# Graph-network kernel: bounded scatters, loads issued ahead of the store, merged one-hots, and message parts kept as upper halves of 32-bit words

## The chip, the cores and the metric

The kernel runs on one core of one Trainium2 chip, as one launch. The metric is the device time of that launch in microseconds (us), as the median of several runs. The engines are PE (TensorE, with PEld for its weight loads), DVE (VectorE), ACT (ScalarE), POOL (GpSimd) and SP (SyncE, which here only issues DMAs).

## The reference, cut to what matters

Four graph layers run one after the other on 6250 nodes of 64 features, each followed by adding to the residual and a layer norm. The 206250 edges (`src`, `dst`) come sorted by `dst`.

```python
# layer 0: hypergraph convolution, twice (relu between): gather, segment sum by edge index, gather, segment sum by node
# layer 1 (pass 4 of the kernel):
h = relu(concat([edges, nodes[receivers], nodes[senders]]) @ We1 + be1)     # one row of 128 per edge
agg = segment_sum(h @ We2 + be2, receivers)
new_nodes = relu(concat([agg, nodes]) @ Wn1 + bn1) @ Wn2 + bn2
# layer 2 (pass 5):
msg = sigmoid(k[dst] + q[src]) * v[src]                                     # one row of 64 per edge
out = segment_sum(msg, dst) + x @ W_skip + b_skip
# layer 3 (pass 6): normalized neighbour sum
```

All of it is float32. The kernel multiplies on PE in bfloat16, with each float32 value split into three bfloat16 parts (high, middle, low) whose products are added in float32.

## The kernel before, in words

The nodes are 49 blocks of 128. A **window** is the block of 128 target nodes whose edges are handled together; there are 49 (`NB`). In each window every edge gets a **slot**: a source block (49 of them) and a place 0 to 127 in it. So gathers and segment sums become matmuls with one-hot matrices of 128 x 128. A **chunk** is seven source blocks (`CH` = 7), so a window has seven chunks (`NC` = 7) and a pass 343.

The stages, in order of time:

1. **Placing the edges** (`place_edges`), window by window: DVE compares and ranks, PE counts, ACT copies. It leaves in `SD` and `slot_rows` the source and target number of every slot, and in `sidx_w` the row of DRAM tensor `feat_slot` to which each edge's features go.
2. **Counts** (`make_counts`): for each chunk DVE builds two one-hots from `sd4` (`one_hots`, L1768 to L1774, two instructions), PE multiplies them into two count matrices (L988), ACT and DVE copy these out (L1343, L1347, L1783), and SP stores them to DRAM (`cnt_t`, `cnt_s`), 3.1 MB a window.
3. **Layer 0**: three products with those counts, loaded again by SP (L519) through a ring of seven buffers (L1052, L1089).
4. **Pass 4** (layer 1) and **pass 5** (layer 2), both by `slots(k)`, with a node stage after each.
5. **Pass 6**: one more product of the counts, and the end.

**The scatters.** `feat_slot` is 307328 rows of 64 floats, filled with zeros by seven DMAs of SP (L490) while the edges are placed. Beside stages 1 to 3 POOL brings the edge features in: per window four loads of nine features for each of 128 partitions (`fetch`, L731, 288 KB each, two buffers) and 36 indirect DMAs (L753), each of which scatters 128 rows of 256 bytes to `feat_slot`. Nothing limits how many are in flight. A `fetch` into a buffer waits until all scatters out of it have landed; it stands after the third scatter of a chunk of nine. Ahead of window 10 POOL waits for the last count matrix (L775). The scatters count up two semaphores, one for each buffer. Pass 4 needs window w of `feat_slot` before its window w (L553).

**One chunk of a slot pass.** SP loads the slot numbers of the chunk, repeated to all 128 partitions, into `selS[c]` and `selT[c]` (L559), in pass 4 also the features `fslot[c]` (L562). DVE turns the two into one-hots in place (`select_rows`, L1951, L1952) and builds a third, `sumT[c]`, the other way round (`select_sums`, L1965). PE transposes the features (L1120, pass 4) and adds up in PSUM, per source block, three products with `selS` and three with `selT` (`meet`, L1137, L1141), in pass 4 also two of the features (L1148). Then the messages are made and split. In pass 4: ACT writes relu of PSUM twice, as float32 in `hid` and as bfloat16, the high part, in `parts3` (L1434, L1435); DVE subtracts (`residual`, L1985); ACT converts the rest, the middle part (L1443); DVE subtracts again, the low part (`last_part`, L1995). In pass 5: ACT's sigmoid (L1438), DVE's product (`gate`, L1979), ACT's high part (L1441), DVE's residual, ACT's middle part, and the low part on POOL (L685). At last PE adds the three parts by target, seven matmuls of 384 or 192 columns (`add_up`, L1161). PE's loop runs `transpose` for chunk c, `meet` for chunk c-2 and `add_up` for chunk c-4; DVE handles the messages of chunk c-2 around the one-hots of chunk c. Once a window ACT and DVE add the two halves of the sum into `ystage` (L1449, L2004 to L2008) and SP stores it (L567).

**The order on SP** in a slot pass is written out: all loads of window w, each behind the semaphore that says that `meet` of the same chunk of window w-1 is done, then the store of window w-1, which waits for DVE's last addition, then the next window's loads:

```python
load(0)
with sp.Fori(1, NB) as w:
    load(w)
    store(w - 1)
store(NB - 1)
```

## Time and profile before

| | us |
|---|---|
| median of three timed runs | 5509.07 |
| lowest and highest | 5475.67, 5522.33 |
| span of the profiled execution | 7358.4 |
| another time of the profiled execution | none recorded |
| PE busy in the span | 4866.3 (66%) |
| DVE, ACT, POOL busy | 3454.7, 2501.9, 2368.3 |

The span is one execution taken by the hardware profiler. It is a third longer than the timed runs, so its stretches have to be read one by one before a duration is carried over to them. "Busy" is time in which an engine executes instructions; waits, branches and the issue of DMAs are not in it.

### The profile page before, as it was taken

Reading aid. Unit: us, or ns where it says so; the run is one execution under the profiler, and the core shown is the slowest. Engines: PE = TensorE matmul, PEld = TensorE weight load, DVE = VectorE, ACT = ScalarE, POOL = GpSimd, SP = SyncE. Lnnn points to the kernel's source line nnn. Section 1 sums busy time; section 2 is a strip of 40 time slices with the busy share of each in tenths; the row PEclk is TensorE's granted clock in tenths of the full one; section 3 lists DMA queues with packets and bytes.
Section 4 is the critical chain, followed back from the end, with each engine's and each line's share of the span. In section 5 each row is a group of like instructions: output and inputs, shape, how many; then the busy total and the mean of one; then the engine's idle time right before and its main releaser. Section 6 shows DMA issues by size and latency. Waiting matters only on the chain.

```text
span 7358.4 us, 157880 instructions
## 1 busy us (share of the span) xinstructions
PE 4866.3 (66%) x61948; PEld 4161.5 (57%) x61948; DVE 3454.7 (47%) x5668; ACT 2501.9 (34%) x3821; POOL 2368.3 (32%) x2387
## 2 busy tenths in 40 slices
PE   2773599623332223328959999999999758877857
PEld 2662488511220112117948888878878657777757
DVE  7992488200000000001046666666666468888842
ACT  1332499200000000000035555555555345555520
POOL 0787400577777777771000000000000013333310
PEclk9666799755555555558979999999999779999989
DMA  7963477722332222327933343443433144444457
GB/s 150 222 140 103 165 290 287 236 74 89 108 111 75 81 88 93 110 88 312 389 123 118 125 132 116 129 129 114 135 122 121 46 157 144 141 144 148 150 193 306
DMA packets 802722, 1103.68 MB, mean 150 GB/s; under 512 B 428155, under 2 KB 708081, under 8 KB 794988
## 3 DMA queue, kind: packets, MB, share of 16 engines
q1 hardware_dynamic: 721658, 986.29, 41.0%
q0 software_dynamic: 73696, 111.71, 5.3%
q8 instruction: 270, 4.42, 0.2%
q10 hardware_dynamic: 7056, 0.91, 0.1%
q14 instruction: 42, 0.34, 0.0%
HBM read 788.30 MB, written 314.35 MB: 150 GB/s over the span
## 4 chain that ended last, share of the span: by engine, by line
PE 35%; issue 26%; another core or an unknown queue 13%; DVE 9%; ACT 5%; DMA 5%; POOL 4%; SPq 2%; DVEq 0%; POOLq 0%; ACTq 0%
PE PS L1052 8%; POOL arena L685 4%; PE PS L1137 4%; PE PS L1141 4%; PE PS L1161 4%; PE PS L1089 4%; PE PS L1148 4%; DMA arena<-feat_slot 3%; PE PS L988 2%; PE PS L1120 2%; DVE arena L1726 1%; ACT arena L1343 1%; PE PS L827 1%; ACT arena L1347 1%
## 5 line engine op out<-in xcount | busy, mean ns | idle before, releaser
L753 POOL DMA_INDIRECT feat_slot<-SK,sidx_p x1764 | 1855.7, 1052 | 1060.5 <-issue 1039.8
L1137 PE MATMUL PS<-arena 128*128 128x128 bf16 x14406 | 1471.6, 222 | 271.6 <-DVE arena L1965 269.2
L1052 PE MATMUL PS<-arena 128*128 128x192 bf16 (+1 forms) x7203 | 832.8, 266 | 1028.1 <-issue 908.2
L1141 PE MATMUL PS<-arena 128*128 (+2 forms) x14406 | 1437.7, 209 | 1.9
L685 POOL TENSOR_TENSOR arena<-arena 128x448 bf16<-128x448 f32 x343 | 360.6, 1051 | 3349.2 <-ACT arena L1443 3349.2
L1052 PEld LDWEIGHTS PS<-arena 128*128 128x128 bf16 x7203 | 648.4, 103 | 1213.5 <-issue 1099.1
L1137 PEld LDWEIGHTS PS<-arena 128*128 128x128 bf16 x14406 | 976.9, 99 | 348.9 <-issue 170.6
L1141 PEld LDWEIGHTS PS<-arena 128*128 128x128 bf16 x14406 | 971.9, 100 | 4.3
L1985 DVE TENSOR_TENSOR arena<-arena 128x896 f32<-128x896 f32 (+1 forms) x686 | 588.3, 858 | 544.9 <-ACT arena L1435 540.1
L1443 ACT ACTIVATE arena<-arena 128x896 bf16<-128x896 f32 (+1 forms) x686 | 523.8, 764 | 634.4 <-DVE arena L1985 634.4
L1161 PE MATMUL PS<-arena 128*128 128x384 bf16 (+1 forms) x4802 | 705.8, 287 | 7.8 <-POOL arena L685 4.0
L1089 PE MATMUL PS<-arena 128*128 128x192 bf16 x2401 | 289.2, 266 | 368.4 <-issue 367.8
L988 PE MATMUL PS<-arena 128*128 128x128 bf16 x4802 | 363.0, 226 | 221.4 <-ACT arena L1343 125.7
L1161 PEld LDWEIGHTS PS<-arena 128*128 128x128 bf16 x4802 | 392.6, 98 | 162.0 <-DVE arena L1995 4.6
L1862 DVE TENSOR_SCALAR arena<-PS 128x448 f32<-128x448 f32 x7 | 4.4, 625 | 1002.0 <-remote 643.9
L1089 PEld LDWEIGHTS PS<-arena 128*128 128x128 bf16 x2401 | 214.0, 103 | 443.6 <-issue 441.8
L988 PEld LDWEIGHTS PS<-arena 128*128 128x128 bf16 x4802 | 300.5, 101 | 273.4 <-issue 110.7
L1995 DVE TENSOR_TENSOR arena<-arena 128x896 bf16<-128x896 f32 x343 | 374.6, 1092 | 147.2 <-ACT arena L1443 142.8
L1965 DVE TENSOR_TENSOR arena<-sd,iota 128x896 bf16<-128x896 bf16 x686 | 424.8, 619 | 3.4
L1833 DVE TENSOR_REDUCE arena<-PS 128x128 f32<-128x384 f32 (+1 forms) x84 | 38.5, 505 | 820.6 <-PE PS L1052 499.8
L1148 PE MATMUL PS<-wtwo,arena 64*128 64x128 f32 x4802 | 399.6, 287 | 0.0
L1343 ACT ACTIVATE arena<-PS 128x896 bf16<-128x896 f32 x343 | 311.6, 927 | 215.3 <-remote 159.4
(238 smaller groups left out, 6438.0 us busy)
## 6 DMA issues: line engine op xcount, KB each, us to landing
arena<-slot_rows SPq DMA_DIRECT2D x1372, 224.0 KB, 4.5
arena<-cnt_t SPq DMA_DIRECT2D x147, 896.0 KB
arena<-cnt_t SPq DMA_DIRECT2D x147, 672.0 KB
feat_slot<-zero SPq DMA_DIRECT2D x7, 10976.0 KB, 54.0
cnt_t<-arena SPq DMA_DIRECT2D x49, 1568.0 KB
cnt_s<-arena SPq DMA_DIRECT2D x49, 1568.0 KB
arena<-feat_slot SPq DMA_DIRECT2D x343, 224.0 KB, 5.1
SK<-in_edge_attr_dram POOLq DMA_DIRECT2D x196, 288.0 KB
```

Source lines behind the costliest of these rows:

```text
L685: pool.tensor_tensor(parts3[i][:, 2 * n:3 * n], hid[i][:, 0:n], parts3[i][:, n:2 * n], ALU.subtract)\
L753: pool.indirect_dma_start(feat_slot, bass.IndirectOffsetOnAxis(ap=sidx_p[odd][:, n:n + 1].bitcast(u32), axis=0), fwin[h][:, t * D:(t + 1) ...
L988: last = nc.tensor.matmul(to[:, cut], one[:, cut], two[:, cut], start=True, stop=True)
L1052: last = nc.tensor.matmul(PS[:, at:at + w3], ring[u % RING][:, of:of + P], esplit[:, (i * CH + w) * w3:(i * CH + w + 1) * w3], start=u == ...
L1089: last = nc.tensor.matmul(PS[:, i * 512:i * 512 + w3], ring[u % RING][:, of:of + P], psplit2[:, b * w3:(b + 1) * w3], start=b == 0, stop=b ...
L1137: last = nc.tensor.matmul(PS[:, to:to + P], selS[c][:, cut], qsplit[:, (b * 3 + s) * H:(b * 3 + s + 1) * H], start=s == 0 and (k != 4 or j ...
L1141: last = nc.tensor.matmul(PS[:, to:to + w_], selT[c][:, cut], dsplit[:, bass.ds(w * (3 * w_) + s * w_, w_)], start=False, stop=k != 4 and ...
L1148: last = nc.tensor.matmul(PS[:, to:to + P], fT[i][rows, pair_of[j] * P:(pair_of[j] + 1) * P], wtwo[rows, :], start=False, stop=True, skip_ ...
L1161: last = nc.tensor.matmul(o, sumT[c][:, j * P:(j + 1) * P], parts[:, :, place_of[j] if k == 4 else j, :], start=c in (0, 4) and j == 0, st ...
L1443: nc.scalar.activation(parts3[i][:, n:2 * n], hid[i][:, 0:n], ACT.Copy).then_inc(msg_mid, 1)
L1965: V.tensor_tensor(sumT[c].rearrange("p (b s a) -> p b s a", b=CH, a=4), sum4[:, c * CH * 4:(c + 1) * CH * 4].rearrange("p (b s a) -> p b s ...
L1985: V.tensor_tensor(hid[i][:, 0:CH * w_], hid[i][:, 0:CH * w_], parts3[i][:, 0:CH * w_], ALU.subtract)\
```

## The change

The edits fall into five groups.

**Scatters.** At most `LIVE` = 4 are in flight: scatter n of a window counts up semaphore n % 4 and waits ahead of that for the scatter before it on the same semaphore. `fetch` stands after the fifth scatter of nine and waits for the same scatters as before. The wait for the count matrices ahead of window 10 is gone. The zero fill writes rows of 448 floats out of a wider `zero` tile instead of 64.

**One-hots of the counts.** The slots are kept in the order (chunk, source or target, block) instead of (source or target, chunk, block), so that both one-hots of a chunk are neighbours and one DVE instruction makes them.

**Slot loads.** By the same order both slot rows of a chunk come in one DMA into `sel_c[c]` (3.5 KB a partition), and one DVE instruction makes one-hots of them.

**Order on SP.** Two windows are loaded first; from then on the store of window w-2 is issued after the fifth chunk's load of window w.

**Message parts.** `hid` has room for three float32 parts. Each part is read as the upper 16 bits of its float32 words (`upper`, a bfloat16 view with a step of two), so no converting copy is made: ACT writes the message (relu) or its gate once, DVE subtracts the upper half of part 1 to get part 2, and DVE or POOL the upper half of part 2 to get part 3. PE reads the `upper` view as its moving operand in `add_up`.

```diff
+LIVE = 4
+PUTS = WT // LIVE
+ZW = 448
+PAIR = 2 * CH
@@ tiles
-        ohs_c = [carve(19 + 1.75 * c, CH * P, bf16) for c in range(NC)]
-        oht_c = [carve(31.25 + 1.75 * c, CH * P, bf16) for c in range(NC)]
+        hot_c = [carve(19 + 3.5 * c, PAIR * P, bf16) for c in range(NC)]
+        ohs_c = [hot[:, 0:CH * P] for hot in hot_c]
+        oht_c = [hot[:, CH * P:PAIR * P] for hot in hot_c]
-        selS = [carve(73.5 + 1.75 * c, CH * P, bf16) for c in range(NC)]
-        selT = [carve(85.75 + 1.75 * c, CH * P, bf16) for c in range(NC)]
+        sel_c = [carve(73.5 + 3.5 * c, PAIR * P, bf16) for c in range(NC)]
+        selS = [sel[:, 0:CH * P] for sel in sel_c]
+        selT = [sel[:, CH * P:PAIR * P] for sel in sel_c]
-        hid = [carve(122.5 + 8.75 * i, CH * P) for i in range(2)]
-        parts3 = [carve(126 + 8.75 * i, 3 * CH * P, bf16) for i in range(2)]
+        hid = [carve(122.5 + 10.5 * i, 3 * CH * P) for i in range(2)]
+        upper = [h.bitcast(bf16).rearrange("p (n two) -> p n two", two=2)[:, :, 1] for h in hid]
@@ SP, zero fill
-                sp.dma_start(z, zero[:, 0:D].rearrange("p (a f) -> p a f", a=1).to_broadcast((P, FROWS // NC // P, D)))\
+                sp.dma_start(z, zero[:, :].rearrange("p (a f) -> p a f", a=1).to_broadcast((P, rows, ZW)))\
@@ SP, slots
-                def load(w):
-                    if k == 4:
-                        for h in range(2):
-                            sp.wait_ge(feat_put[h], w * (FCH // 2 * FT * 16) + FCH // 2 * FT * 16)
+                def load(w, between=None):
                     for c in range(NC):
-                        if not isinstance(w, int):
+                        if not isinstance(w, int) or w > 0:
                             sp.wait_ge(pre_made, w * NC + (m * GB + c + 1 - NC))
-                        for kk, to in ((0, selS[c]), (1, selT[c])):
-                            row = slot_rows[bass.ds(w, 1), kk * NB + c * CH:kk * NB + (c + 1) * CH, :]
-                            sp.dma_start(to, row.rearrange("a k s -> a (k s)").to_broadcast((P, CH * P))).then_inc(slot_in[c], 16)
+                        rows = slot_rows[bass.ds(w, 1), c * PAIR:(c + 1) * PAIR, :]
+                        sp.dma_start(sel_c[c], rows.rearrange("a k s -> a (k s)").to_broadcast((P, PAIR * P))).then_inc(slot_in[c], 16)
                         if k == 4:
+                            if c == 0:
+                                for i in range(LIVE):
+                                    sp.wait_ge(feat_put[i], w * (PUTS * 16) + PUTS * 16)
...
+                        if between is not None and c == 4:
+                            store(between)
...
                 load(0)
-                with sp.Fori(1, NB) as w:
-                    load(w)
-                    store(w - 1)
+                load(1)
+                with sp.Fori(2, NB) as w:
+                    load(w, w - 2)
+                store(NB - 2)
                 store(NB - 1)
@@ POOL, last part of pass 5
-                        pool.wait_ge(msg_mid, w * NC + (GB + c + 1))
-                        pool.tensor_tensor(parts3[i][:, 2 * n:3 * n], hid[i][:, 0:n], parts3[i][:, n:2 * n], ALU.subtract)\
+                        pool.wait_ge(msg_res, w * NC + (GB + c + 1))
+                        pool.tensor_tensor(hid[i][:, 2 * n:3 * n], hid[i][:, n:2 * n], upper[i][:, n:2 * n], ALU.subtract)\
@@ POOL, put_features
                         n = c * FT + t
+                        i = n % LIVE
+                        if not isinstance(w, int) or w > 0 or n >= LIVE:
+                            pool.wait_ge(feat_put[i], w * (PUTS * 16) + n // LIVE * 16)
+                            pool.nop(nofuse=True)
                         pool.indirect_dma_start(
...
-                            .then_inc(feat_put[h], 16)
-                        if t == 2 and c < FCH - 1:
+                            .then_inc(feat_put[i], 16)
+                        if t == 4 and c < FCH - 1:
                             fetch(w, c + 1)
...
-            with pool.Fori(3, 5) as i:
-                put_features(i * 2, 0)
-                put_features(i * 2 + 1, 1)
-            pool.wait_ge(cs_made, NB * NC)
-            with pool.Fori(5, NB // 2) as i:
+            with pool.Fori(3, NB // 2) as i:
@@ PE, add_up
-                    parts = parts3[(c + odd) % 2][:, 0:3 * CH * w_].rearrange("p (s j f) -> p s j f", s=3, j=CH)
+                    parts = upper[(c + odd) % 2][:, 0:3 * CH * w_].rearrange("p (s j f) -> p s j f", s=3, j=CH)
@@ ACT, messages
                     if k == 4:
-                        nc.scalar.activation(hid[i], PS[:, at:at + CH * P], ACT.Relu).then_inc(msg_made, 1)
-                        nc.scalar.activation(parts3[i][:, 0:n], PS[:, at:at + CH * P], ACT.Relu).then_inc(pre_free, 1)
+                        nc.scalar.activation(hid[i][:, 0:n], PS[:, at:at + CH * P], ACT.Relu).then_inc(pre_free, 1)
...
-                        act.wait_ge(pre_free, w * NC + (GB + c + 1))
-                        nc.scalar.activation(parts3[i][:, 0:n], hid[i][:, 0:n], ACT.Copy).then_inc(msg_hi, 1)
-                    act.wait_ge(msg_res, w * NC + (m * GB + c + 1))
-                    nc.scalar.activation(parts3[i][:, n:2 * n], hid[i][:, 0:n], ACT.Copy).then_inc(msg_mid, 1)
@@ DVE, make_counts
-                    for k, to in ((0, ohs_c[c]), (1, oht_c[c])):
...
+                    V.tensor_tensor(
+                        hot_c[c].rearrange("p (b s a) -> p b s a", b=PAIR, a=4),
...
@@ DVE, slots
-                    V.tensor_scalar(selS[c], selS[c], pnum1[:, 0:1], None, ALU.is_equal)
-                    V.tensor_scalar(selT[c], selT[c], pnum1[:, 0:1], None, ALU.is_equal)
+                    V.tensor_scalar(sel_c[c], sel_c[c], pnum1[:, 0:1], None, ALU.is_equal)
...
-                    dve.wait_ge(*((pre_free, w * NC + (c + 1)) if k == 4 else (msg_hi, w * NC + (c + 1))))
-                    V.tensor_tensor(hid[i][:, 0:CH * w_], hid[i][:, 0:CH * w_], parts3[i][:, 0:CH * w_], ALU.subtract)\
-                        .then_inc(msg_res, 1)
+                    dve.wait_ge(pre_free, w * NC + (m * GB + c + 1))
+                    V.tensor_tensor(hid[i][:, n:2 * n], hid[i][:, 0:n], upper[i][:, 0:n], ALU.subtract).then_inc(msg_res, 1)
...
-                    dve.wait_ge(msg_mid, w * NC + (m * GB + c + 1))
-                    V.tensor_tensor(parts3[i][:, 2 * n:3 * n], hid[i][:, 0:n], parts3[i][:, n:2 * n], ALU.subtract)\
+                    dve.wait_ge(msg_res, w * NC + (m * GB + c + 1))
+                    V.tensor_tensor(hid[i][:, 2 * n:3 * n], hid[i][:, n:2 * n], upper[i][:, n:2 * n], ALU.subtract)\
```

## Rows read from the trace of the kernel before

**Rows 1.** The profile page: its head.

```profile
span 7358.4 us, 157880 instructions
```

**Rows 2.** Busy time by stretch: stretch, length, then busy us of each engine.

```profile
0.00:556.00 556.00, 327.83 (x4321) 268.23 (x4321) 498.78 (x573) 161.82 (x491) 314.43 (x226) 0.78 0.77 170
556.00:840.00 284.00, 81.67 (x711) 67.27 (x712) 49.16 (x85) 54.49 (x66) 211.19 (x222) 0.58 0.30 94
840.00:1331.00 491.00, 461.72 (x6488) 425.11 (x6485) 437.86 (x749) 460.71 (x573) 0.14 (x1) 0.99 0.73 288
1331.00:3683.00 2352.00, 950.95 (x7342) 687.68 (x7343) 95.92 (x228) 30.50 (x50) 1481.99 (x1597) 0.61 0.42 140
3816.00:5740.00 1924.00, 1794.05 (x22706) 1559.24 (x22707) 1234.14 (x1886) 1112.11 (x1403) 0.00 (x0) 0.97 0.40 126
5952.00:7060.00 1108.00, 879.74 (x16807) 804.37 (x16807) 916.60 (x1911) 566.20 (x1079) 360.59 (x343) 0.99 0.46 144
```

**Rows 3.** Busy time by stretch of line 988 alone (PE, PEld, clock, DMA).

```profile
840.00:1331.00 491.00, 309.50 (x4318) 258.40 (x4315) 0.99 0.73 288
```

**Rows 4.** Busy time in the last product, which runs beside nothing.

```profile
7120.00:7320.00 200.00, 200.00 (x2390) 199.67 (x2391) 16.47 (x36) 4.76 (x10) 0.00 (x0) 0.99 0.96 386
```

**Rows 5.** Timeline of pass 4 (start, us, engine, line; idle before), and PE's waits.

```profile
4632.98 0.36 SPq L567 DMA_DIRECT2D acc<-ystage  x1
4635.03 0.33 SPq L562 DMA_DIRECT2D arena<-feat_slot  x1
4640.13 0.65 PE L1120 MATMUL PS<-ident,arena 128*128 128x128 f32 x4 [3.26 <-DMA arena<-feat_slot]
4645.80 1.31 PE L1161 MATMUL PS<-arena 128*128 128x384 bf16 x7
4646.94 0.60 PE L1120 MATMUL PS<-ident,arena 128*128 128x128 f32 x4
4652.06 0.60 PE L1120 MATMUL PS<-ident,arena 128*128 128x128 f32 x4
...
PE PS L1120 <- DMA arena<-feat_slot: 126.0, 47, 3.8
```

**Rows 6.** Timeline of pass 5, one chunk.

```profile
6501.97 0.53 ACT L1438 ACTIVATE arena<-PS 128x448 f32<-128x448 f32 x1
...
6502.53 0.62 DVE L1979 TENSOR_TENSOR arena<-arena,PS 128x448 f32<-128x448 f32 x1 [0.54 <-ACT arena L1438]
...
6503.18 0.58 ACT L1441 ACTIVATE arena<-arena 128x448 bf16<-128x448 f32 x1 [0.69 <-DVE arena L1979]
...
6503.43 0.45 DVE L1952 TENSOR_SCALAR arena<-arena,pnum 128x896 bf16<-128x896 bf16 x1
...
6503.79 0.62 DVE L1985 TENSOR_TENSOR arena<-arena 128x448 f32<-128x448 f32 x1
...
6504.33 0.62 DVE L1965 TENSOR_TENSOR arena<-sd,iota 128x896 bf16<-128x896 bf16 x1
...
6504.45 0.58 ACT L1443 ACTIVATE arena<-arena 128x448 bf16<-128x448 f32 x1 [0.69 <-DVE arena L1985]
...
6504.93 0.53 ACT L1438 ACTIVATE arena<-PS 128x448 f32<-128x448 f32 x1
...
6505.01 0.34 PE L1137 MATMUL PS<-arena 128*128 128x128 bf16 x3 [0.43 <-DVE arena L1965]
```

**Rows 7.** Line 753 alone by stretch, and a wait of POOL's.

```profile
200.00:556.00 356.00, 290.60 (x166) 0.69 0.79 177
556.00:840.00 284.00, 195.44 (x195) 0.58 0.30 94
...
POOL SK L731 <- DMA feat_slot<-SK,sidx_p: 17.7, 5, 12.9
```

**Rows 8.** A scatter in the first stage, and DVE's longest group of lines.

```profile
215.01 2.58 POOL L753 DMA_INDIRECT feat_slot<-SK,sidx_p  x1 [0.30 <-issue]
...
L1705 DVE TENSOR_TENSOR arena<-arena,iota 128x4608 bf16<-128x4608 bf16 x49 | 125.0, 2552 | 0.0
```

54 lines of the change are left out of this document (27 added, 27 removed).

## The prediction, made before the result was known

> **What bounds the kernel now.** I read the page's head first, then busy time by stretch, then one window of each slot pass as a timeline, then POOL's scatters. The profiled execution spans 7358.4 us, for which no other time is recorded; the three timed runs have a median of 5509.07 [rows 1]. The span is 1849 us longer, so I first ask where. The stretches show it [rows 2]: placing the edges takes 556 us; then come 491 us in which the counts stage does 4318 matmuls at L988, at 98 a window 44 windows of 11.14 us [rows 3], and ahead of them 284 us in which it does the other 5; layer 0 takes 2352 us; then 133 us to the start of pass 4, which takes 1924; 212 us to pass 5, which takes 1108; 298 us to the end. Both odd stretches are those in which scatters run beside big loads or stores: the DMA engines are 0.30 and 0.42 busy, against 0.73 in the free counts stretch. A product that runs free takes 200 us at 386 GB/s [rows 4]. Undisturbed, the counts stage would take 49 x 11.14 = 546 and layer 0 three products and some 16 us around them, 616. The whole is then 556 + 546 + 616 + 133 + 1924 + 212 + 1108 + 298 = 5393, 116 below the median. So the timed runs hold at most about 116 us of this disturbance where the profile has 1964, and the sum below, made on the span's stages, is taken off the median too.
>
> **Pass 4** is PE's: 1794 of 1924 us busy [rows 2]. A chunk takes 5.12 us from one transpose group to the next, PE without a gap; 49 windows x 7 would take 1756. The rest is at the window's first chunk. SP issues the store of `ystage` at 4632.98, which it was waiting for, and only then, at 4635.03, the feature load that PE needs; it lands when PE has stood 3.26 us. Such waits are 126.0 us in 47 of them. The next transposes start 6.81 us after these, the ones behind those 5.12 later [rows 5]: after the stall the same matmuls also run 1.69 us longer.
>
> **Pass 5** has no idle PE clock (0.99) but PE is busy 880 of 1108 us and DVE 917. A chunk's period is 2.96 us and is one closed chain between ACT and DVE [rows 6]: sigmoid at 6501.97, gate at 6502.53, high part at 6503.18, residual at 6503.79, middle part at 6504.45, next sigmoid at 6504.93. PE waits there for L1965, which DVE issues late because its gate waits for that sigmoid.
>
> **The change, part by part.**
>
> *Loads ahead of the store.* In both passes the loads of a window no longer stand behind the store of the window before: SP issues load c as soon as matmul group c of the last window is done, five chunks (over 13 us) before it is read, against a landing of 5.1 us [rows 5]. SP gets one row load per chunk instead of two, 343 fewer in each pass; the load that replaces them has their bytes. The store of window w-2 moves behind load 4 of window w. Its wait (DVE's last addition of w-2) is long over there, so nothing queues behind it; DVE needs that store gone only in the next window's fifth chunk, some five chunks on, so its landing is covered. Pass 4 loses the 126 us and part of the slow matmuls: 1924 - 1756 = 168, less some 20 us of filling at the start that stays. **-150**, bounds -120 and -168. What comes next is PE itself.
>
> *Message parts as upper halves.* In pass 4 ACT drops two of its three message operations per chunk (L1435, L1443). ACT (1112 of 1924 us) and DVE (1234) are off the path there [rows 2], so I cost this at nothing; PE hides it. In pass 5 it opens the chain: ACT keeps only the sigmoid. DVE per chunk by the starts is now 1.26 for gate and two selects, 0.54 for the residual and 0.62 for the one-hot, 2.42 [rows 6]; two selects 0.36 each become one, for which I take 0.60 (bounds 0.36, a free second half, and 0.72): 2.3. A PE chunk is the 2.96 less the 0.43 it waits, 2.53. Per window PE needs 17.7 us (17.95 by its busy time), DVE 7 x 2.3 and, of its 917/49 = 18.7 busy us, the 1.8 that are not chunks (the sums of the window before, a small copy), 17.9. The gate of chunk c still needs PE's group c and a 0.53 us sigmoid, so DVE is at most a chunk ahead and its extra 1.8 us costs PE about 1 us. I take 19.0 against 1108/49 = 22.6: **-175**, of which I book **-165** for the start. Bounds: -220 if PE alone remained, 0 if another wait of the same length follows.
>
> *PE reads with a step of two.* No row shows such a read. From below the price is nothing, the contiguous rate: seven 384-column matmuls at L1161 take 1.14 us to the next start, 163 ns each. From above I take the nearest 4-byte read, the f32 transposes, four of 128 columns in 0.60 us [rows 5], 1.17 ns a column against 0.42; that would be 287 ns more per matmul, 2401 times, 689 us in pass 4 alone. By it this term is nothing; no run shown here tests it.
>
> *Merged one-hots in the counts stage.* ACT is busy 461 of 491 us [rows 2] and bounds it; DVE gives up one start per chunk, which may fill part of the 0.68 us (6% of 11.14) that ACT idles per window. **-10**, bounds 0 and -33.
>
> *Four scatters in flight, no hold.* The added waits want scatter n-4 landed. POOL's edge load waits for the scatters of the chunk before, the last of them three scatters old, and it is shown waiting in 5 of 196 cases, 17.7 us [rows 7], so a wait for the fourth is rare. Wait and nop themselves I take as free. The hold at window 10 goes, so POOL scatters through the rest of the counts stage and ends earlier. Nobody waits for it: scattering at the 284 us stretch's pace (195, 1.46 us each) ends at 200 + 1764 x 1.46 = 2775, while pass 4 wants its last window at 556 + 546 + 616 + 133 + 47 x 35.8 = 3534. Edge loads are fetched two scatters later; that may stall POOL a few hundred us in all, inside the same slack. What it does to the neighbours: at best the 116 us vanish, at worst the freed half of the counts stage takes as much again, +116. **-15**.
>
> A rule speaks against scattering there. The trace first: while DVE was 0.9 busy placing edges, a scatter was busy 1.75 us and came every 2.14 (166 in 356 us), some of 2.58, which is L1705's length; beside a nearly idle DVE it was busy 1.00 [rows 7, 8]. The Trainium skill (SBUF — State Buffer, Who interferes with whom) has descriptor generation blocked by DVE's two-port modes, and infers that `tensor_tensor`, which L1705 is, does not block it. By the skill the scatters would pass through the counts stage at 1.46 us, by the trace at some 2.1; I follow the trace, and the scatters end some 250 us later, which the slack covers.
>
> *The zero fill* in rows of 1792 bytes instead of 256 is done before the edges are placed in both; DVE bounds that stage (0.90 busy). Nothing, cover: DVE's 499 us.
>
> **Sum**: -150 -165 -10 -15 = -340. On the span 7018, on the median 5169; I say 5170. A measurement here can tell about 1% from no change (the three runs span 47 us).
>
> **Rivals.**
> *A, as forecast*, 5030 to 5290: 0.55.
> *B, pass 5 and the DMA give less*: the chain in pass 5 re-forms over PE, sigmoid and gate near 21.5 us a window (-55), and scatters cost the counts stage up to 116. 5509 - 150 - 55 + 80 = 5384; for it, DVE is already busiest in that pass. 5290 to 5454: 0.25.
> *C, the scatters become pass 4's gate*: at 2.14 us each throughout they end at 200 + 1764 x 2.14 = 3975 instead of by 3534, 441 us late: 5169 + 441 = 5610. It decides from (3534 - 200)/1764 = 1.89 us a scatter. The limit of four makes it likelier (a landing over 7 us would do); against it are 1.00 us scatters wherever DVE is idle, as in layer 0. 0.08, half of it over +1%.
> *D, the stepped read is slow; slower than before*: place L1161, twice the time per column. 163 ns more x 2401 = +391 in pass 4; pass 5's PE chunk grows by 7 x 0.08 (half the columns) to 3.10, 21.7 us a window and 22 with waits, which leaves -30 there. 5509 - 150 + 391 - 30 - 25 = 5695. It decides when the step costs over 205/391 of that, 0.22 ns a column. 0.09.
> *E*, more than forecast (all disturbance gone, under 5030): 0.03.
>
> **Numbers.** 5170. The range takes A and B and leaves out about 2 in 10: 5030 to 5440. Faster by over 1% (under 5454): A, B and E, 0.82; within 1%, B's tail and half of C, 0.06; slower, D and the rest of C, 0.12.
>
> **What would show it.** Pass 4: no wait of L1120 on `feat_slot` after the first window, period 35.8; seven L1161 of 384 columns still in 1.14 us (right) or near 2.3 (D). Pass 5: ACT one operation per chunk, period 2.5 to 2.7, PE over 0.9 busy. Scatters: durations of 1.0 to 2.1 us, the last one before pass 4's window 40; SP waiting at `feat_put` would be C. Counts: 11.0 to 11.2 us a window where stores are not held up.

## The result: 159 us faster, where 340 were forecast

| | before | after |
|---|---|---|
| median of the timed runs, us | 5506.11 (5475.67 to 5522.33) | 5346.74 (5312.17 to 5361.59) |
| ratio, with its 95% interval | 1 | 0.9707 (0.9668 to 0.9747) |
| span of the profiled execution | 7358.4 | 5310.0 (its own time 5312.17) |

The kernel is faster. Its time lies inside the stated range and in that of rival B, 177 us above the 5170 that were forecast. Busy time by stretch of the changed kernel, as in [rows 2]: placing the edges, counts, layer 0, pass 4, pass 5.

```profile
0.00:556.00 556.00, 325.44 (x4321) 265.41 (x4321) 498.82 (x573) 163.34 (x492) 310.11 (x224) 0.78 0.50 169
556.00:1118.00 562.00, 512.67 (x7203) 471.90 (x7203) 471.65 (x509) 516.25 (x646) 353.40 (x299) 0.98 0.86 312
1118.00:1790.00 672.00, 632.99 (x7350) 622.74 (x7350) 87.68 (x211) 25.88 (x41) 389.43 (x420) 0.97 0.99 387
1923.00:3745.00 1822.00, 1784.28 (x22974) 1531.41 (x22974) 1173.84 (x1564) 535.27 (x735) 1161.71 (x1032) 1.00 0.52 165
3908.00:5010.00 1102.00, 909.92 (x16807) 851.97 (x16807) 875.90 (x1569) 201.37 (x393) 411.96 (x343) 0.96 0.43 144
```

Against [rows 2] pass 4 went from 1924 to 1822 and pass 5 from 1108 to 1102 (forecast -165, measured -6). My stretch for pass 4 of before ended 6 us ahead of its last transposes (at 5745.7), and this one ends 16 behind them; from first to last transpose it is 1927.8 before and 1803.5 after, -124 where -150 was forecast. The two stretches that ran over in the profile of before are ordinary ones now. In pass 5 ScalarE's busy time fell from 566 to 201 us and VectorE's from 917 to 876; the pass got shorter by only 5 us (1091.2 to 1086.6 from GpSimd's first to its last part).

The two passes together hold 129 of the 159 us. The other 30 lie outside them, where the same code differs by about as much from one profiled kernel to the next (last section).

**Pass 4.** What PE and SyncE wait for in it:

```profile
PE PS L1131 <- DMA arena<-feat_slot: 70.1, 3, 68.1
PE PS L1131 <- issue: 32.9, 22, 1.9
```

```profile
SPq L559 <- PE PS L1159: 1276.2, 319, 8.1
SPq L572 <- DVE ystage L2012: 20.4, 1, 20.4
```

Line 1131 is the transpose that was L1120. Its waits for features [rows 5] are gone but for the filling of the first window (68.1 of 70.1 us), and SyncE now waits at nearly every load (319 times) for PE to free its buffer, as it should. Two things took some of it back. About once in two windows PE stands some 1.5 us ahead of its first transposes with nothing recorded that releases it, and the seven 384-column matmuls of L1172 take 1.36 us, 1.21 from start to start, where they took 1.31 and 1.14:

```profile
2619.47 0.65 PE L1131 MATMUL PS<-ident,arena 128*128 128x128 f32 x4 [1.42 <-issue]
2623.52 1.36 PE L1172 MATMUL PS<-arena 128*128 128x384 bf16 x7
2624.73 0.60 PE L1131 MATMUL PS<-ident,arena 128*128 128x128 f32 x4
2629.90 0.60 PE L1131 MATMUL PS<-ident,arena 128*128 128x128 f32 x4
```

**Pass 5.** The timeline that answers to [rows 6] (L1448 sigmoid, L1983 gate, L1990 residual, L1969 one-hots, L691 GpSimd's last part, L1172 PE's last product, L1965 the copy and L1455 the sum at a window's end):

```profile
4306.79 0.54 ACT L1448 ACTIVATE arena<-PS 128x448 f32<-128x448 f32 x1 [2.64 <-PE PS L1172]
...
4309.25 0.77 PE L1172 MATMUL PS<-arena 128*128 128x192 bf16 x7
4309.29 1.25 POOL L691 TENSOR_TENSOR arena<-arena 128x448 f32<-128x448 f32 x1 [1.09 <-DVE arena L1990]
4310.11 0.33 ACT L1455 ACTIVATE y<-PS 128x192 f32<-128x192 f32 x1 [2.79 <-PE PS L1172]
4310.34 0.54 ACT L1448 ACTIVATE arena<-PS 128x448 f32<-128x448 f32 x1
4310.91 0.62 DVE L1983 TENSOR_TENSOR arena<-arena,PS 128x448 f32<-128x448 f32 x1 [1.17 <-ACT arena L1448]
...
4312.05 0.62 DVE L1990 TENSOR_TENSOR arena<-arena 128x448 f32<-128x448 f32 x1
4312.58 0.35 DVE L1965 COPY sd<-SD 128x196 bf16 x1
4312.74 0.93 POOL L691 TENSOR_TENSOR arena<-arena 128x448 f32<-128x448 f32 x1 [2.21 <-DVE arena L1990]
4312.97 1.19 DVE L1969 TENSOR_TENSOR arena<-sd,iota 128x896 bf16<-128x896 bf16 x1
4314.29 0.34 PE L1148 MATMUL PS<-arena 128*128 128x128 bf16 x3 [1.88 <-DVE arena L1969]
```

ScalarE's chain is gone. The sigmoid now waits for L1172, PE's last product, and not for its own chunk's group of products (`meet`). In `messages` the sigmoid of chunk c waits not only for group c but, with two message buffers, for `agg_made` of chunk c-2, and PE runs that product behind group c. What the prediction read as "PE's group c and a 0.53 us sigmoid" is PE's group c, 0.77 us of product, and the sigmoid.

The second finding is in PE's clock. First PE's timeline around one of the long waits, then the busy time of the engines in stretches of 2 and 3 us before, in, and behind it (PE, PEld, DVE, ACT, POOL; then the clock):

```profile
4288.43 0.77 PE L1172 MATMUL PS<-arena 128*128 128x192 bf16 x7
4291.30 0.34 PE L1148 MATMUL PS<-arena 128*128 128x128 bf16 x3 [2.10 <-DVE arena L1969]
...
4294.29 1.31 PE L1172 MATMUL PS<-arena 128*128 128x192 bf16 x7
```

```profile
4286.00:4289.00 3.00, 3.00 (x62) 2.96 (x59) 1.34 (x3) 0.88 (x2) 1.05 (x1) 1.00 0.47 140
4289.00:4291.00 2.00, 0.20 (x3) 0.00 (x0) 1.97 (x4) 0.54 (x1) 0.93 (x1) 1.00 0.59 210
4292.00:4295.00 3.00, 3.00 (x39) 2.94 (x37) 1.36 (x3) 0.00 (x0) 1.25 (x1) 0.51 0.00 1
4296.00:4299.00 3.00, 2.43 (x51) 2.20 (x48) 2.69 (x5) 0.72 (x2) 0.96 (x1) 1.00 0.52 176
```

PE stands 2.1 us, and the granted clock behind that is 0.51, the 1.2 GHz level, for some 3 us: 39 matmuls fit where 62 did. Not every long wait does this. In 895 us of pass 5, about 40 windows, the trace has 40 waits of 1.88 to 2.10 us, and the clock fell behind 23 of them, each time for some 3 us; it fell behind no shorter one, and nowhere in such a stretch of before, whose longest wait is 1.4 us. The mean clock there was 1.00 before and is 0.96 now. Waits and busy time there:

```profile
4068.00:4963.00 895.00, 743.86 (x13705) 696.40 (x13702) 713.33 (x1279) 163.51 (x320) 336.55 (x280) 0.96 0.44 145
```

```profile
PE PS L1148 <- DVE arena L1969: 147.9, 157, 2.1
```

A window has 343 matmuls, so the stretch holds 13705/343 = 39.96 windows: PE busy 18.62 us and waiting 3.70 in each. A stretch of before of the same length holds 40.02 windows:

```profile
6055.00:6950.00 895.00, 716.17 (x13727) 655.00 (x13724) 748.23 (x1560) 461.60 (x881) 294.37 (x281) 1.00 0.47 145
```

```profile
PE PS L1137 <- DVE arena L1965: 175.0, 221, 1.4
```

17.90 busy and 4.37 waiting. The change took 0.67 us of waiting out of a window and put 0.72 us of PE's busy time in. The waits became fewer (157 for 221) but longer (up to 2.1 for 1.4), and the clock that fell behind them is enough for the 0.72: 23 times 3 us at half the pace is some 35 us in 40 windows, 0.9 in each (an estimate from these rows). That is why the pass hardly moves.

### The profile page after: what moved, and what is told of

It reads as the page before. It is cut to its first block, busy times and chain, and to the rows that moved or that the text cites. A ratio compares the mean times of both kernels' runs of the same rounds, so it can differ in the third digit from the quotient of the medians.

```text
span 5310.0 us, 156295 instructions
## 1 busy us (share of the span) xinstructions
PE 4488.9 (85%) x61948; PEld 4050.7 (76%) x61948; DVE 3313.7 (62%) x4639; ACT 1543.4 (29%) x2449; POOL 2721.3 (51%) x2387
## 4 chain that ended last, share of the span: by engine, by line
PE 52%; issue 18%; DVE 10%; DMA 8%; POOL 7%; ACT 4%; SPq 1%; DVEq 0%; POOLq 0%; ACTq 0%
PE PS L1063 9%; PE PS L1172 8%; PE PS L1148 8%; PE PS L1152 8%; PE PS L1159 7%; POOL arena L691 7%; PE PS L1131 3%; DMA arena<-cnt_t 3%; PE PS L1100 3%; PE PS L999 2%; DVE arena L1732 2%; ACT arena L1354 2%; ACT arena L1358 1%; DVE arena L1774 1%; PE PS L1008 1%
## 5 line engine op out<-in xcount | busy, mean ns | idle before, releaser
L768 POOL DMA_INDIRECT feat_slot<-SK,sidx_p x1764 | 2153.8, 1221 | 907.5 <-issue 507.3
L1148 PEld LDWEIGHTS PS<-arena 128*128 128x128 bf16 x14406 | 977.8, 99 | 295.4 <-issue 184.3
L691 POOL TENSOR_TENSOR arena<-arena 128x448 f32<-128x448 f32 x343 | 412.0, 1201 | 1178.1 <-DVE arena L1990 1178.1
L1990 DVE TENSOR_TENSOR arena<-arena 128x896 f32<-128x896 f32 (+1 forms) x686 | 586.1, 854 | 639.7 <-ACT arena L1445 639.6
L1152 PEld LDWEIGHTS PS<-arena 128*128 128x128 bf16 x14406 | 967.7, 99 | 4.8
L1172 PE MATMUL PS<-arena 128*128 128x384 bf16 (+1 forms) x4802 | 741.8, 294 | 4.4 <-POOL arena L691 2.3
L1063 PE MATMUL PS<-arena 128*128 128x192 bf16 (+1 forms) x7203 | 616.2, 248 | 102.8 <-DVE arena L1828 62.4
L1063 PEld LDWEIGHTS PS<-arena 128*128 128x128 bf16 x7203 | 607.1, 98 | 110.4 <-DVE arena L1828 62.6
L1172 PEld LDWEIGHTS PS<-arena 128*128 128x128 bf16 x4802 | 401.8, 98 | 176.0 <-POOL arena L691 2.7
L1956 DVE TENSOR_SCALAR arena<-arena,pnum 128x1792 bf16<-128x1792 bf16 x686 | 470.8, 686 | 10.8 <-DMA arena<-feat_slot 6.6
L1969 DVE TENSOR_TENSOR arena<-sd,iota 128x896 bf16<-128x896 bf16 x686 | 451.4, 658 | 3.4
L1434 ACT ACTIVATE arena<-PS 128x512 f32<-128x512 f32 x343 | 204.8, 597 | 839.9 <-PE PS L1159 778.7
L1448 ACT ACTIVATE arena<-PS 128x448 f32<-128x448 f32 x343 | 186.6, 544 | 757.2 <-PE PS L1172 740.0
L1445 ACT ACTIVATE arena<-PS 128x896 f32<-128x896 f32 x343 | 314.7, 917 | 205.4 <-PE PS L1172 205.4
L1999 DVE TENSOR_TENSOR arena<-arena 128x896 f32<-128x896 f32 x343 | 371.9, 1084 | 0.1
L1159 PEld LDWEIGHTS PS<-wtwo,arena 64*128 64x128 f32 x4802 | 332.9, 187 | 35.6
L1774 DVE TENSOR_TENSOR arena<-sd,iota 128x1792 bf16<-128x1792 bf16 x343 | 352.0, 1084 | 9.5 <-DMA slot_rows<-arena 9.5
L999 PEld LDWEIGHTS PS<-arena 128*128 128x128 bf16 x4802 | 288.0, 98 | 79.9 <-DVE arena L1774 29.3
```

The source lines that it names most:

```text
L691: pool.tensor_tensor(hid[i][:, 2 * n:3 * n], hid[i][:, n:2 * n], upper[i][:, n:2 * n], ALU.subtract)\
L768: pool.indirect_dma_start(feat_slot, bass.IndirectOffsetOnAxis(ap=sidx_p[odd][:, n:n + 1].bitcast(u32), axis=0), fwin[h][:, t * D:(t + 1) ...
L999: last = nc.tensor.matmul(to[:, cut], one[:, cut], two[:, cut], start=True, stop=True)
L1063: last = nc.tensor.matmul(PS[:, at:at + w3], ring[u % RING][:, of:of + P], esplit[:, (i * CH + w) * w3:(i * CH + w + 1) * w3], start=u == ...
L1148: last = nc.tensor.matmul(PS[:, to:to + P], selS[c][:, cut], qsplit[:, (b * 3 + s) * H:(b * 3 + s + 1) * H], start=s == 0 and (k != 4 or j ...
L1152: last = nc.tensor.matmul(PS[:, to:to + w_], selT[c][:, cut], dsplit[:, bass.ds(w * (3 * w_) + s * w_, w_)], start=False, stop=k != 4 and ...
```

## Experiments

The names: `u_` and `o_store` are the changed kernel with one part undone, `b_order` is the kernel before with one part added, and the kernels with `n` go on from the changed one. Pass 4 is measured below from its first to its last transpose, pass 5 from GpSimd's first to its last part; the stretches above are 18.5 and 15.4 us longer. Before they are 1927.8 and 1091.2. Each ratio is to runs of before taken beside that kernel's; their medians are 5506 to 5523 us.

| kernel | ratio to before (95%) | median us | pass 4 | pass 5 |
|---|---|---|---|---|
| after | 0.9707 (0.9668 to 0.9747) | 5347 | 1803.5 | 1086.6 |
| u_parts | 0.9650 (0.9627 to 0.9672) | 5330 | 1788.8 | 1091.2 |
| u_scatters | 0.9664 (0.9624 to 0.9705) | 5345 | 1799.7 | 1086.8 |
| u_order | 0.9947 (0.9917 to 0.9977) | 5481 | 1942.0 | 1089.3 |
| o_store | 0.9932 (0.9904 to 0.9960) | 5467 | 1925.6 | 1088.1 |
| b_order | 0.9674 (0.9641 to 0.9707) | 5342 | 1796.6 | 1091.0 |
| n1_seven_buffers | 0.9531 (0.9509 to 0.9553) | 5261 | 1800.3 | 1014.1 |
| n4_copies_seven | 0.9635 (0.9605 to 0.9665) | 5316 | 1791.1 | 1072.9 |
| n5_mixed | 0.9558 (0.9515 to 0.9601) | 5263 | 1786.8 | 1024.4 |
| n6_reduce_two | 0.9541 (0.9482 to 0.9600) | 5260 | 1799.4 | 997.6 |
| n3_one_reduce | 0.9376 (0.9344 to 0.9408) | 5169 | 1799.5 | 916.1 |
| n8_copies_reduce | 0.9558 (0.9507 to 0.9610) | 5255 | 1788.9 | 1013.9 |
| n7_sums_on_act | 0.9318 (0.9266 to 0.9369) | 5130 | 1803.7 | 870.1 |

### What gave pass 4 its time: the order, and in it the store

**u_order**: SyncE's order as before, the rest as changed.

```
+                def load(w):
+                    if k == 4:
+                        for i in range(LIVE):
+                            sp.wait_ge(feat_put[i], w * (PUTS * 16) + PUTS * 16)
...
-                load(1)
-                with sp.Fori(2, NB) as w:
-                    load(w, w - 2)
-                store(NB - 2)
+                with sp.Fori(1, NB) as w:
+                    load(w)
+                    store(w - 1)
```

> The changed kernel with SyncE's order alone as before: the loads of window w and the wait for its scatters in front of the store of window w-1, and only one window loaded ahead. Theory: pass 4 owes its 102 us to this order, by which the features of a window are asked for before PE is done with the last: pass 4 goes from 1822 back to 1900-1925, pass 5 stays within 20 us of 1102; the kernel 5430-5460 (0.985 to 0.99 of before). Rival, the limit of four scatters and the smaller DMA traffic gave pass 4 its time: pass 4 stays within 20 us of 1822, the kernel at 5335-5370.

Measured: pass 4 1942.0, 0.9947. The theory holds in kind: pass 4 is 138.5 us longer than in after, more than the 124 by which after differs from before. It is more than the theory's interval too: as a stretch pass 4 would be some 1960 us, where at most 1925 were expected, and the kernel's 5481 lies above 5460. SyncE's and PE's waits in 1500 us of it:

```profile
SPq L570 <- DVE ystage L2009: 782.1, 38, 20.7
...
PE PS L1128 <- issue: 79.6, 19, 5.3
PE PS L1128 <- DMA arena<-feat_slot: 24.6, 19, 2.3
```

SyncE stands 20 us of a window in front of the store, which waits for VectorE's sum of the window before; the next window's first loads come only then, and PE meets them late. Of PE's 104 us only 24.6 are put down to the features, the rest to nothing; those waits come at the same transposes, 19 of each, and after has only 30.3 us of the second kind in as many us, so most of them are probably the same thing; no run shows it.

**o_store**: the store alone goes back behind all loads of the next window, with one window loaded ahead; the wait for scatters stays where the change put it.

```
-                        if between is not None and c == 4:
-                            store(between)
...
-                load(1)
-                with sp.Fori(2, NB) as w:
-                    load(w, w - 2)
-                store(NB - 2)
+                with sp.Fori(1, NB) as w:
+                    load(w)
+                    store(w - 1)
```

> The changed kernel with the store alone put back: one window loaded ahead, the store of window w-1 behind all loads of window w; the wait for the scatters stays in front of the first feature load. Theory: SyncE stood 785 us of 1500 in front of that store (wait for the sum of the window, which comes in the fifth chunk of the next), and that is what made the next window's loads late; so all of the order's effect comes back: pass 4 at 1920-1945 us from its first to its last transpose (1803.4 as changed, 1942.0 with the old order), the kernel 5465-5490 (0.990 to 0.996). Rival, half of it is the wait for the scatters in front of chunk 0's rows: pass 4 at 1850-1890, the kernel 5400-5440.

Measured: 1925.6 and 0.9932. The place of the store, and with it the number of windows loaded ahead, brings back 122 of u_order's 138.5 us, and the two kernels' times do not differ clear of noise. The 16 us between the two profiles would be the wait for the scatters, if they are more than chance.

**b_order**: the kernel before with the changed order and nothing else.

```
+                        if k == 4:
+                            if c == 0:
+                                for h in range(2):
+                                    sp.wait_ge(feat_put[h], ...)
...
+                        if between is not None and c == 4:
+                            store(between)
...
+                load(1)
+                with sp.Fori(2, NB) as w:
+                    load(w, w - 2)
```

> The kernel before with SyncE's order alone changed: two windows loaded ahead, the wait for a window's scatters in front of its first feature load only, the store of window w-2 after the fifth chunk's load. Theory: nearly the whole gain of the change is this: 130 to 160 us, 5355-5385 (0.971 to 0.977 of before); pass 4 at 1785-1800 us from its first to its last transpose, pass 5 at 1091. Rival, the order pays only together with the other edits (the wider zero fill, merged loads, the missing hold): 60 us or less, 5450 or more.

Measured: 0.9674 (0.9641 to 0.9707), pass 4 1796.6, pass 5 1091.0, slightly under the expected time. This one edit has the whole gain of the change: added to it, merged chunks, message parts, limit of four and zero fill bring nothing that the runs can tell from zero.

The ratios do not add up all the same. With the old order those other edits leave 0.9932 and 0.9947, 29 to 37 us, although the two passes together are 5 us shorter (o_store) and 12 us longer (u_order) than before. If the profiled passes are taken off the median times, the rest is 30 to 50 us shorter than in before in after and in all four kernels of this section, also in b_order, whose code outside the passes is that of before. So before holds some tens of microseconds outside the passes that each of these kernels has lost; no run shows where.

**u_scatters**: no limit, two semaphores, earlier fetches, and the hold, as before.

```
-                        if not isinstance(w, int) or w > 0 or n >= LIVE:
-                            pool.wait_ge(feat_put[i], ...)
-                            pool.nop(nofuse=True)
...
+            pool.wait_ge(cs_made, NB * NC)
```

> The changed kernel with the scatters alone as before: no limit of four in flight, two semaphores, fetches after the third scatter of a chunk, and the wait for the end of the counts in front of window 10. Theory: the scatters are off the path that sets the end in both; pass 4 stays within 20 us of 1822 after its first window, and the kernel within 50 us of 5347, while the profiled run may be longer than the timed ones, as it was before. Rival, the limit is what made pass 4 faster, since scatters without a limit fill the queues that the loads of pass 4 need: pass 4 goes back to 1900 or more and the kernel to 5430 or more.

Measured: 0.9664, pass 4 1799.7: as the theory says. But the profiled run was 5354.4 us long, not inflated: neither here nor in b_order (5344.3), where all scatters are as before, did the stretches of [rows 2] come back. The 1965 us or so that the profile of before holds in them beyond an undisturbed run are so far a property of one execution, and their cause stays open.

### What held pass 5: two loops, the window's end, and the clock

**n1_seven_buffers**: one message buffer for each chunk of a window.

```
-                    if later(w, c, 2):
-                        act.wait_ge(agg_made, w * NC + (m * GB + c - 1))
+                    if k == 5 and later(w, 0, 1):
+                        act.wait_ge(agg_made, w * NC + (m * GB + c + 1 - NC))
```

> The changed kernel, with one edit in pass 5: seven message buffers, one for each chunk of a window, in place of two, so that the sigmoid of chunk c (L1448) waits for the last product (L1172) of the same chunk one window back and not for that of chunk c-2. Theory: the loop gate - select - residual - select sums (2.3 us on VectorE) - PE's group (1.80) - PE's last product of chunk c-2 (0.77) - sigmoid (0.55), 5.5 us for two chunks, holds pass 5 at 22.35 us a window; without the wait in it the loop is 4.7 us for two chunks and PE's own 18.6 us of work a window becomes the bound: pass 5 falls from 1102 us to 960-1020, the kernel from 5347 to 5210-5270 (0.946 to 0.957 of before). Rival 1, VectorE with slower operations, or the clock, bounds it: pass 5 stays at 1085-1105, the kernel at 5330-5350. Rival 2, GpSimd's last part of 1.20 us (L691) bounds it: the same, since that part is unchanged.

Measured: pass 5 1014.1 (some 1030 as a stretch, 10 over the expected interval), the kernel 5261, 0.9531, as expected; both rivals had no gain. But a window still takes 895/(14697/343) = 20.9 us (14697 matmuls in 895 us) for PE's 18.0. ScalarE's waits show that a product is still in its way: the copy of the first half's sum (L1465 here) stands in ScalarE's queue ahead of a sigmoid and waits for chunk 3's product:

```profile
ACT arena L1458 <- PE PS L1159: 567.5, 257, 5.5
ACT y L1465 <- PE PS L1179: 151.0, 43, 3.7
```

**u_parts**: message parts as before (ScalarE's copies, contiguous reads), the rest as changed.

```
-                    parts = upper[...][:, 0:3 * CH * w_]
+                    parts = parts3[...][:, 0:3 * CH * w_]
...
+                        nc.scalar.activation(parts3[i][:, 0:n], hid[i][:, 0:n], ACT.Copy).then_inc(msg_hi, 1)
+                    act.wait_ge(msg_res, w * NC + (m * GB + c + 1))
+                    nc.scalar.activation(parts3[i][:, n:2 * n], hid[i][:, 0:n], ACT.Copy).then_inc(msg_mid, 1)
```

> The changed kernel with the message parts alone as before: ScalarE's copies of the high and middle part are back, and PE reads bf16 values that lie side by side; merged chunks, order of loads and scatters stay as changed. Theory (the wait for the last product of chunk c-2 is in the loop of pass 5, and the stepped read costs PE 5%): pass 4 falls by 0 to 40 us from 1822 where PE's last product goes back to 163 ns a matmul, pass 5 stays within 15 us of 1102; the kernel 5300-5360. Rival 1, the parts are what made VectorE's and GpSimd's operations slow enough to eat the gain forecast for pass 5: pass 5 falls by 80 us or more, to 5270 or less. Rival 2, taking ScalarE's copies away is what made pass 4 faster: pass 4 goes back to 1900 or more, the kernel to 5430.

Measured: pass 4 1788.8, pass 5 1091.2, the kernel 5330: the theory; neither rival. The parts, which carried the forecast for pass 5, bring 5 us there and cost 15 in pass 4. PE's busy time and waits in 895 us of pass 5 are those of before (715.87 and 175.2 us against 716.17 and 175.0), although the select is one instruction here.

**n4_copies_seven**: the edits of u_parts and of n1_seven_buffers together.

> Message parts as before in both passes (ScalarE's two copies back) and seven message buffers in pass 5, on the changed kernel. Theory (two loops of almost the same length hold pass 5: ScalarE's in the order gate 0.54, high copy 0.58, residual 0.54, middle copy 0.58, sigmoid 0.53, 2.97 us a chunk with gaps, and the one through the wait for the product of chunk c-2; the change took out the first, the buffers take out the second): with the first back, the buffers bring nothing: pass 5 stays at 1080-1095 us from its first to its last GpSimd part (1091.2 in the run with the old parts), the kernel at 5310-5345. Rival, the buffers alone are what counts: pass 5 falls to 1014-1040 as with seven buffers and the new parts, the kernel to 5240-5270.

Measured: 1072.9 in pass 5, 5316. 7 us under the theory's interval for the pass, and far from the rival. VectorE's gates go at ScalarE's period again, 2.96 us, and not at a loop over chunk c-2:

```profile
4306.45 0.62 DVE L2001 TENSOR_TENSOR arena<-arena,PS 128x448 f32<-128x448 f32 x1 [0.54 <-ACT arena L1462]
4309.41 0.62 DVE L2001 TENSOR_TENSOR arena<-arena,PS 128x448 f32<-128x448 f32 x1 [0.54 <-ACT arena L1462]
4312.37 0.62 DVE L2001 TENSOR_TENSOR arena<-arena,PS 128x448 f32<-128x448 f32 x1 [0.54 <-ACT arena L1462]
```

So both loops were there in before, ScalarE's in front. The new parts alone bring 5 us (1091.2 to 1086.6), the buffers alone 18 (to 1072.9), both together 77 (to 1014.1).

**n3_one_reduce**: n1 and, in pass 5, the sum at the window's end as one instruction.

```
+                    if k == 5:
+                        at = 3072 + odd * 512
+                        V.tensor_reduce(ystage[:, 0:w_], PS[:, at:at + 3 * w_].rearrange("p (s f) -> p f s", s=3), AX.X, ALU.add)\
+                            .then_inc(zb_kept, 1)
+                        return
```

ScalarE's copy L1455 is left out for it, and PE adds up all seven chunks in one bank.

> Seven message buffers in pass 5, and there the sum at the end of a window as one VectorE instruction (three parts summed straight from one PSUM bank a window, banks alternating) in place of a ScalarE copy and three dependent VectorE instructions (0.35, 0.57, 0.23 us, 1.13 from start to start with what follows). Theory: the 2.8 us a window for which PE still waits on the one-hots in the run with seven buffers come from VectorE's extra work at the window's end, 1.13 us of it for that sum: pass 5 falls from 1014 to 960-985 us, the kernel to 5205-5235. Rival, PE's wait there comes from the clock and from the slow one-hots beside GpSimd's part (1.19 us once a window): pass 5 stays at 1005-1015, the kernel at 5255-5265.

Measured: pass 5 916.1, the kernel 5169, 0.9376: twice the expected gain, 98 us instead of 29 to 54. The direction was right, the price was not. In 895 us (16286/343 = 47.5 windows):

```profile
3945.00:4840.00 895.00, 840.52 (x16286) 786.86 (x16284) 807.74 (x1425) 182.32 (x334) 401.43 (x334) 1.00 0.51 169
```

```profile
PE PS L1155 <- DVE arena L1985: 47.1, 47, 1.1
```

PE is busy 17.70 us and waits 0.99 a window, against 17.99 and 2.80 in n1. So 0.29 us are faster matmuls, with the clock at 1.00 where it was 0.98, and 1.81 are shorter waits. VectorE's own saving, from start to start, is 1.13 - 0.27 = 0.86 of them. The other 0.95 I put down to ScalarE's queue, now free of the copy; no run has the single sum with the copy left in, so this share is argued.

**n6_reduce_two**: the single sum, but two buffers.

> The changed kernel with the single sum instruction in pass 5 and two message buffers as they were. Theory: the wait for the product of chunk c-2 still holds the chunks between the window ends at 5.5 us for two; only the window's end gets shorter, by 0.8 us and some of the long waits behind it: pass 5 1035-1060 us from its first to its last GpSimd part (1086.6 as changed, 1014 with seven buffers, 916 with both), the kernel 5290-5325. Rival, the two edits are independent and add: 988 us, the kernel 5245-5255.

Measured: 997.6 and 5260. The theory missed by 37 us or more; the rival's sum was 988. So the two edits nearly add. The loop of the theory is there all the same: 5.58 us for two chunks,

```profile
4324.26 0.62 DVE L1989 TENSOR_TENSOR arena<-arena,PS 128x448 f32<-128x448 f32 x1 [0.91 <-ACT arena L1452]
4326.73 0.61 DVE L1989 TENSOR_TENSOR arena<-arena,PS 128x448 f32<-128x448 f32 x1
4329.84 0.62 DVE L1989 TENSOR_TENSOR arena<-arena,PS 128x448 f32<-128x448 f32 x1 [0.83 <-ACT arena L1452]
```

7 x 2.79 = 19.5 us a window; the 20.4 measured (997.6/49) leave 0.9 for its end. What I had not counted is the clock: no wait is over 1.1 us any more, the clock is 1.00, and PE is busy 778.09/43.8 = 17.77 us a window instead of 18.62. Of the 1.8 us a window that the single sum saves here, 0.85 are faster matmuls and 1.03 shorter waits.

**n8_copies_reduce**: old parts, seven buffers, single sum.

> Message parts as before (ScalarE's copies back), seven message buffers and the single sum instruction in pass 5. Theory: ScalarE's loop of 2.97 us a chunk holds it: 7 x 2.97 = 20.8 us a window and up to 0.8 for its end, pass 5 1015-1055 us, the kernel 5250-5300; against 916 and 5169 with the changed parts, so that the changed parts are worth 100 us or more once buffers and sum no longer hide it. Rival, the copies are not the bound and the parts are worth nothing here either: pass 5 915-935, the kernel 5165-5190.

Measured: 1013.9 and 5255, 0.9558: the theory, at the lower end. ScalarE's period is bare here (L1466 sigmoid, L1469 and L1471 the copies):

```profile
4301.56 0.53 ACT L1466 ACTIVATE arena<-PS 128x448 f32<-128x448 f32 x1
4302.78 0.58 ACT L1469 ACTIVATE arena<-arena 128x448 bf16<-128x448 f32 x1 [0.69 <-DVE arena L2007]
4304.04 0.58 ACT L1471 ACTIVATE arena<-arena 128x448 bf16<-128x448 f32 x1 [0.69 <-DVE arena L2013]
4304.53 0.53 ACT L1466 ACTIVATE arena<-PS 128x448 f32<-128x448 f32 x1
```

2.97 from sigmoid to sigmoid, seven times 20.8, and 1013.9/49 = 20.7. With buffers and sum in place the changed parts are worth 98 us (1013.9 to 916.1). So they have a gain, behind two other bounds, but 98 us and not the 165 that the forecast gave them. The other 77 of the 175 us between u_parts and n3 (1091.2 and 916.1) come from buffers and sum without them.

**n7_sums_on_act**: n3, and the columns for the one-hots repeated by ScalarE into two buffers; in pass 5 VectorE no longer copies them.

```
+                def repeat_sums(w, odd):
+
+                    if later(w, 0, 2 * NC):
+                        act.wait_ge(sel_made, w * NC + (m * GB - NC))
+                    nc.scalar.activation(sd4[odd][:, 0:NB * 4].rearrange("p (c j a) -> p c j a", c=NC, a=4),
...
-                    if c == 0:
+                    four = sd4[odd] if k == 5 else sum4
+                    if c == 0 and k == 5:
+                        dve.wait_ge(sum4_made, w + (m * NB + 1))
+                    if c == 0 and k == 4:
```

> Seven message buffers, the single sum instruction, and in pass 5 the repeated sum columns written by ScalarE into two buffers in place of VectorE's copy (0.35 us) at the start of each window. Theory: that copy pushes the one-hots behind it into GpSimd's part, where they take 1.19 us and not 0.62, and PE then waits 1.08 us once a window; without it PE waits for nothing and its own 18.0 us a window are left: pass 5 875-895 us (916 with the copy), the kernel 5125-5150 (0.930 to 0.935). Rival, another one-hot or the select meets GpSimd's part then and takes twice its time: pass 5 stays at 910-920, the kernel at 5165-5175.

Measured: pass 5 870.1, just under the expected 875, the kernel 5130, 0.9318. The one-hots and PE in 850 us:

```profile
L1998 DVE TENSOR_TENSOR arena<-sd,iota 128x896 bf16<-128x896 bf16 x334 | 207.0, 620 | 0.0
```

```profile
3980.00:4830.00 850.00, 842.50 (x16351) 788.24 (x16347) 771.55 (x1383) 193.72 (x381) 415.74 (x334) 1.00 0.55 181
```

The one-hots take 620 ns on the mean, where n3 has 698; a window takes 17.83 us, and PE is busy 0.99 of it. This kernel is faster than before (0.9318, 0.9266 to 0.9369) and than the changed one (0.9707).

**n5_mixed**: n1, with the old parts in pass 4 only.

> Message parts as before in pass 4, as changed in pass 5, with seven message buffers in pass 5. Theory: the effects are each in their pass and add: pass 4 at 1789 us from its first to its last transpose (1803.4 in the changed kernel), pass 5 at 1014; the kernel 5235-5255 (0.949 to 0.953). Rival, the difference of 15 us in pass 4 is not from PE's stepped read but from chance between executions: pass 4 stays at 1800, the kernel at 5255-5265.

Measured: pass 4 1786.8 as expected, but pass 5 1024.4, 10 us over n1's, and the whole 0.9558 against n1's 0.9531. The 14 us in pass 4 are the step's (1787 to 1791 in the four kernels with contiguous reads under the new order and merged chunks, 1799 to 1804 in the six with the step; b_order, contiguous but with two selects, 1796.6), but the time of the whole kernel does not show them and lies at the rival's 5255 to 5265: inconclusive for the kernel. The clock accounts for the 10 us in pass 5. In 895 us it fell behind 16 long waits here and behind 10 in n1, with the same code there, and PE is busy 18.17 us a window for 17.99.

## Where the prediction was right and where it failed

- *The sum's base*: the counts stage and layer 0 take 562 and 672 us, where I had 546 and 616 undisturbed, so 72 us more stand there after the change too; b_order, with scatters and fill as before, has 562 and 682. I put them down to the scatters beside these stages, but no run left the scatters out.
- *Scatters -15 and one-hots -10*: outside the two passes the kernel did get some 30 us shorter, but not by these two edits (u_scatters above, and 562 us with and without the merged one-hots). That the -25 of these two terms come near it is luck.
- *Loads ahead of the store, -150*: the mechanism is right, shown from both sides (u_order, o_store, b_order). The feature waits went, 128 us of them (194.4 less the 66.3 of the first window). The slower matmuls went too: PE is busy 1799.9 us in pass 4 of before and 1754.8 in that of b_order, 45 less for the same matmuls, with the clock at 0.97 and 0.99. Against them stand 32.9 us of waits at L1131, which b_order has as well (39.8 in 22) and which the feature waits may have covered, and 15 for the step of two: -124. What PE waits for in these 1.5 us was not explained.
- *Message parts in pass 5, -165*: **the step that failed**, in these words: "The gate of chunk c still needs PE's group c and a 0.53 us sigmoid, so DVE is at most a chunk ahead and its extra 1.8 us costs PE about 1 us." The gate also needed PE's product of chunk c-2. The runs show four things where I had that chain: the sigmoid's wait for this product (n1), ScalarE's copy of the half sum in the sigmoid's queue and the three dependent additions on VectorE (n3 and n6 take out both together), and the clock, which fell behind the longer waits. Measured: -5 as changed. The 19.0 us a window that I named is reached only with n3's two further edits (18.7), and of the 175 us to there the parts have 98.
- *Rival B* had the form of it ("the chain in pass 5 re-forms over PE, sigmoid and gate near 21.5 us a window"), but a window takes 22.2 us (1086.6/49), and the scatters did not cost the 80 us that it adds. Its 5384 comes near the 5347 by errors that cancel: 50 us too much gained in pass 5, 26 too much in pass 4, and some 110 too little outside the passes.
- *The merged select*: 0.60 from start to start, as taken, only where the residual behind it no longer waits for ScalarE; in u_parts it is 0.72, as the two were.
- *Step of two, 0 with 689 as bound*: 1.21 - 1.14 = 0.07 us for seven matmuls, 6%, in pass 4, 10 ns each. Near the lower end, so rival D is out. By the Trainium skill (Advanced Engine Details and Errata, SBUF Cachelines) accesses that hit the same 16-byte line again have full performance, which would put the step at nothing; by the run without the step (u_parts) it is 15 us in pass 4, and the measurement decides.
- *Scatters*: beside a busy VectorE they are as forecast, 1.74 us each. I called a wait for the fourth one back rare: the limit made GpSimd wait 350.9 us in 326 waits from 556 to 3420. The last scatter started at 3416.6, not near 3025, with pass 4 in its window 40; but SyncE never stood at `feat_put` in pass 4, so nobody waited for it. Rival C is out: undoing the limit moves nothing (5345 for 5347).
- *One-hots -10*: not seen. VectorE's busy time fell by 22 us in a stage that ScalarE bounds. *Zero fill 0*: right; the DMA share of the first stage fell from 0.77 to 0.50 and its length stayed 556.

The timed runs of before fit these stages better than my subtraction did: 556 + 562 + 682 + 133 + 1924 + 212 + 1108 + 298, with b_order's counts and layer 0, is 5475, against 5506 measured and the 5393 that I had.

## To carry to other kernels

When a closed chain of waits is taken out of a loop, list every other wait that the same instruction has and everything in its engine's queue ahead of it, and work out each as a loop of its own, before the saving is booked down to the next engine's busy time; here the second loop lay 6% under the first (2.79 against 2.97 us a chunk). Look at a queue's issuer first: one store in front of loads on SyncE was worth all that this change gained in pass 4. And a saving that leaves fewer but longer waits on PE can be given back by its clock; look at the longest wait and not only at the sum.

## What the runs showed of the hardware

- PE's granted clock went from 1.00 to 0.51 behind a wait of 2.1 us, for some 3 us of full work. In 895 us of pass 5 it fell behind 23 of after's 40 waits of 1.88 to 2.10 us and behind none in before, n6 and n8, whose longest waits are 1.4, 1.1 and 0.9 us. PE was busy 0.72 us a window longer than in before for it, and 0.85 longer than in n6, of 22.4.
- One-hots that start while GpSimd's part runs take 1.19 us (48 of them in pass 5 of after), 0.62 otherwise; GpSimd's part takes 0.93 when it starts first and 1.25 when VectorE is ahead, as at 4312.74 and 4309.29 above. The Trainium skill (SBUF — State Buffer, Who interferes with whom) says that a VectorE instruction with two SBUF inputs contends with a GpSimd instruction that reads SBUF, and that the order of issue decides which of the two is held up. The trace agrees, and in n7 no one-hot is slow any more.
- An equal stretch of code can differ by some 25 us between kernels: from the last transpose of pass 4 to the first part of pass 5 took 191 to 195 us in six of the profiled kernels and 214 to 219 in the others, whatever had been changed. The first transpose of pass 4 came at 1925 to 1958 us in all but the profile of before. So a difference of that size between two single profiles in other stretches was not read as an effect.
